# Values of two token blocks by seven quarter products, with running sums of queries, keys and values in PSUM

## What is computed

```python
qkv = x @ w_qkv.T                       # 512 -> 3 * 512
q, k = q*cos + rotate_half(q)*sin, k*cos + rotate_half(k)*sin
keep = (rel >= 0) & (rel < 64)          # window
out = softmax(where(keep, q @ k.T * scale, -inf)) @ v @ w_out.T
x = layernorm(x + out)
fuse = silu((x @ w_gate) * s_gate) * ((x @ w_up) * s_up)
x = layernorm(x + (fuse @ w_down) * s_down)
```

## Time and profile before

| | us |
|---|---|
| median of 3 runs | 1167.48 |
| the three runs | 1166.87, 1167.51, 1167.48 |
| span of the profiled execution, from its first to its last instruction | 1164.2 |

### The profile page before, as it was taken

How to read it: one execution, slowest core, us unless ns; L and a number is a source line. 1 busy time by engine, 2 the same in 40 slices (tenths; PEclk the granted TensorE clock), 3 DMA queues, 4 the chain that set the end, 5 groups by cost and what they waited for, 6 DMA issues and landing times.

```text
span 1164.2 us, 25539 instructions
## 1 busy us (share of the span) xinstructions
PE 1154.0 (99%) x8433; PEld 567.9 (49%) x8433; DVE 984.6 (85%) x2821; ACT 584.4 (50%) x1640; POOL 587.3 (50%) x563
## 2 busy tenths in 40 slices
PE   9999999999999999999999999999999999999998
PEld 4344446444464444644455444554445444464444
DVE  7899998898987899879998899897898988986434
ACT  3953883048820588105880169701686027950330
POOL 0775684156731667326771367613676236752330
PEclk9999999999999999999999999999999999999999
DMA  9999786366562765617656096561964537734000
GB/s 295 173 175 252 137 166 160 66 88 137 111 149 55 110 131 107 145 41 128 132 97 141 37 146 119 101 132 46 155 123 88 131 63 137 120 73 109 19 2 36
DMA packets 352077, 134.80 MB, mean 116 GB/s; under 512 B 309840, under 2 KB 332496, under 8 KB 351952
## 3 DMA queue, kind: packets, MB, share of 16 engines
q1 hardware_dynamic: 334976, 106.86, 49.6%
q0 software_dynamic: 10560, 17.30, 5.1%
q10 hardware_dynamic: 6416, 9.00, 2.1%
HBM read 32.19 MB, written 8.39 MB: 35 GB/s over the span
## 4 chain that ended last, share of the span: by engine, by line
PE 97%; DVE 1%; ACT 1%; issue 1%; POOL 0%; POOLq 0%; DVEq 0%
PE bank L842 61%; PE bank L1058 18%; PE bank L848 10%; PE bank L984 3%; PE bank L964 2%; PE bank L864 1%; PE bank L1080 1%; ACT bank L1243 1%; PE bank L873 0%; PE bank L1069 0%; PE bank L948 0%; DVE wd L1373 0%; ACT wu L1186 0%; DVE ffn_tmp L1530 0%; ACT fuse L1186 0%
## 5 line engine op out<-in xcount | busy, mean ns | idle before, releaser
L842 PE MATMUL bank<-x1T,wg 128*128 128x512 f16 (+1 forms) x1032 | 242.5, 378 | 0.0
L842 PE MATMUL bank<-x1T,wu 128*128 128x512 f16 x1024 | 241.9, 379 | 0.0
L1243 ACT ACTIVATE bank<-bank,neg_max,qk_scale 128x128 f32<-128x128 f32 x512 | 220.5, 435 | 7.8 <-DVE neg_max L1558 6.1
L1058 PE MATMUL bank<-wd,fuse 128*128 128x512 f16 (+2 forms) x1056 | 222.7, 373 | 0.0
L660 POOL TENSOR_TENSOR fuse<-ffn_tmp,fuse 128x512 f16<-128x512 f32 x128 | 149.7, 1170 | 117.5 <-ACT fuse L1186 116.8
L742 POOL TENSOR_TENSOR fuse<-fuse 128x512 f16<-128x512 f32 x116 | 137.7, 1218 | 74.9 <-ACT fuse L1186 72.8
L1058 PEld LDWEIGHTS bank<-wd,fuse 128*128 128x128 f16 x1056 | 101.9, 98 | 118.0
L842 PEld LDWEIGHTS bank<-x1T,wu 128*128 128x128 f16 x1024 | 100.1, 98 | 120.7
L655 POOL TENSOR_TENSOR xT_sb<-probs,xT_sb 128x512 f16<-128x512 f32 x112 | 129.6, 1158 | 44.5 <-ACT xT_sb L1186 44.4
L842 PEld LDWEIGHTS bank<-x1T,wg 128*128 128x128 f16 x1032 | 96.3, 98 | 113.9 <-issue 4.0
L1196 ACT ACTIVATE ffn_tmp<-bank,tanh_scale 128x512 f32<-128x512 f32 x128 | 88.2, 689 | 100.0 <-PE bank L842 76.8
(11 more groups left out here) (235 smaller groups left out, 1621.5 us busy)
## 6 DMA issues: line engine op xcount, KB each, us to landing
v_cross<-v_own SPq DMA_DIRECT2D x64, 128.0 KB, 2.4
out<-x ACTq DMA_DIRECT2D x31, 256.0 KB, 2.0
xT_sb<-xT SPq DMA_DIRECT2D x30, 256.0 KB, 4.1
qkT<-x SPq DMA_DIRECT2D x28, 256.0 KB, 3.8
wg<-w_gate POOLq DMA_DIRECT2D x7, 1024.0 KB, 5.2
wu<-w_up POOLq DMA_DIRECT2D x7, 512.0 KB, 6.0
wqkv<-w_qkvT SPq DMA_DIRECT2D x8, 256.0 KB, 6.3
wg<-w_gate POOLq DMA_DIRECT2D x1, 2048.0 KB, 8.4
```

The lines of the kernel that those rows point to most:

```text
L842: last = pe.matmul(dst, lhsT, rhs, start=(i == 0), stop=(i == len(pairs) - 1))
L1058: last = pe.matmul(dst[:, cols], fuse[:, s, z, rows], wd[:, s, cols], start=(s == 0 and z == 0), stop=(s == STEPS - 1 and z == 1))
L1243: last = act.activation(unit, unit, ACT.Exp, bias=neg_max[:, s % 2, h // 3, h % 3:h % 3 + 1], scale=qk_scale[:, 2:3], accum_out=row_sum[:, ...
```

## The change

Values are now also done by pairs of blocks, seven quarter products of 256 columns for each pair (`values_first` to `values_fourth`), 14 for a tile in place of four plain products. The scheme needs the sums of x that queries and keys already have, and four sums of the value weights. One of them replaces a part of `wqkv` in place; the other three are made once by POOL, stored in a DRAM tensor, `kept_v_weights`, and loaded back by ACT in each tile into the part of `v_cross` that is free between two tiles (`load_v_weights`).

In both schemes some of the seven products now add onto what stands in the bank: PE makes a product, ACT copies it (`keep_first`, `keep_fifth`, `keep_sixth`, `keep_seventh`, and `keep_values_...` with the scale of the values), and the next product is added to it in PSUM. So for queries and keys ACT makes four copies for a pair instead of one, and DVE three sums instead of seven. For values ACT makes four half-width copies for a pair, DVE adds kept part and bank into float32 rows (`add_v`, rows in `y`, `ffn_tmp` and `v_cross`), ACT makes their high half from those rows (`keep_v`), and DVE the low half from rows and high half (`split_v`, both in SBUF). The gate product of step 0 waits for `add_v` 0 and 1, that of step 1 for all four. The first three value products are issued at the end of the body before (`begin_values`), in place of the first block's product. In `first` POOL makes the sums of x for both pairs and those of the weights. Names of sums in `x_sums` and `w_sums` only change places.

```diff
+
         def kept_products(i):
 
-            if i == 0:
-                return rope_other[0], rope_other[1], rope_other[3]
-            return y[:, 0, :], ffn_tmp[:, 0, :], ffn_tmp[:, 1, :]
+            return rope_other if i == 0 else [o_rows[:, n, :] for n in range(NB)]
...
+        def v_places(i):
+
+            front, back = bank32[2 * i], bank32[2 * i + 1]
+            return front[:, 0:HALF_EMB], front[:, HALF_EMB:], back[:, 0:HALF_EMB], back[:, HALF_EMB:]
...
             def cross_v(a, j):
+                if j == 0 and not (isinstance(a, int) and a == 0):
+                    wait(v_product[1], sp, a - 1, V_FOURTH)
+                    sp.sem_inc(passed, 1)
+                    sp.wait_ge(v_weights_kept, 3 * 16)
+                    sp.sem_inc(passed, 1)
                 wait(v_low, sp, a, j)
...
+            def lessen_v_weights():
+                low_left, low_right, high_left, high_right = v_quarters()
+                wait(v_done, pool, 0, NB - 1)
+                pool.tensor_tensor(low_right, low_right, low_left, ALU.subtract).then_inc(v_weights_lessened, 1)
+
+            def add_v_weights():
+                low_left, right_less_left, high_left, high_right = v_quarters()
+                second, third, fourth = (added_v_weights(n) for n in range(3))
+                wait(pv_done, pool, 0, STEPS - 1)
+                pool.wait_ge(v_weights_lessened, 1)
+                pool.tensor_tensor(second, high_right, right_less_left, ALU.subtract).then_inc(v_weights_added, 1)
+                pool.wait_ge(v_weights_added, 1)
+                pool.tensor_tensor(fourth, high_left, second, ALU.subtract).then_inc(v_weights_added, 1)
+                pool.tensor_tensor(third, second, low_left, ALU.subtract).then_inc(v_weights_in[0], 16)
...
-            def project_pair(a, i, first=False):
...
+            def pair_first(a, i):
                 front_low, front_high, back_low, back_high = x_quarters(i)
...
+                done(first_product, quarter(pair_banks(i)[2], front_low, low_even))
...
+            def pair_fifth(a, i):
+                low_even, odd_less_even, high_even, high_odd = w_quarters()
+                pe.wait_ge(w_summed, 4)
+                done(fifth_product, quarter(pair_banks(i)[1], x_sums(i)[:, 1, :, :], odd_less_even))
+
+            def pair_sixth(a, i):
+                wait(products_kept, pe, a - 1, 4 * turn_of(i))
+                done(sixth_product, quarter(pair_banks(i)[2], x_sums(i)[:, 2, :, :], w_sums[:, 1, :, :], True))
+
+            def pair_seventh(a, i):
+                wait(products_kept, pe, a - 1, 4 * turn_of(i) + 2)
+                done(seventh_product, quarter(pair_banks(i)[2], x_sums(i)[:, 0, :, :], w_sums[:, 2, :, :], True))
+
+            def pair_third(a, i):
+                low_even, odd_less_even, high_even, high_odd = w_quarters()
+                wait(products_kept, pe, a - 1, 4 * turn_of(i) + 1)
+                done(qk_done, quarter(pair_banks(i)[1], x_sums(i)[:, 3, :, :], high_odd, True))
+
+            def pair_fourth(a, i):
+                front_low, front_high, back_low, back_high = x_quarters(i)
+                wait(products_kept, pe, a - 1, 4 * turn_of(i) + 3)
+                done(qk_done, quarter(pair_banks(i)[2], back_high, w_sums[:, 0, :, :], True))
+
+            def project_pair(a, i):
                 for j in (2 * i, 2 * i + 1):
                     wait_xT(pe, a, j)
-                if i == 0:
-                    wait(proj_read, pe, a - 1, NB - 1)
-                elif first:
-                    wait(proj_read, pe, a - 1, 1)
-                else:
-                    wait(down_read, pe, a - 2, NB - 1)
-                done(first_product, quarter(front_even, front_low, low_even))
-                if first:
-                    project_o(a - 1, NB - 1, False)
-                    wait(proj_read, pe, a - 1, 2)
-                wait(x_summed, pe, a - 1, 3)
-                pe.wait_ge(w_summed, 3)
-                done(sixth_product, quarter(back_even, sums[:, 1, :, :], w_sums[:, 0, :, :]))
-                pe.wait_ge(w_summed, 4)
...
-            def project_v(a, j, ffn, parts=range(KC)):
...
+            def values_first(a, i):
+                front_low, front_high, back_low, back_high = x_quarters(i)
+                low_left, right_less_left, high_left, high_right = v_quarters()
+                wait(rope_read, pe, a, i)
...
+            def values_fifth(a, i):
+                low_left, right_less_left, high_left, high_right = v_quarters()
...
+                done(v_product[i], quarter(v_places(i)[1], x_sums(i)[:, 1, :, :], right_less_left))
+
+            def values_sixth(a, i):
+                wait(v_products_kept[i], pe, a - 1, 0)
+                wait(v_weights_in, pe, a - 1, 15)
+                done(v_product[i], quarter(v_places(i)[3], x_sums(i)[:, 2, :, :], added_v_weights(0), True))
...
+            def values_second(a, i):
+                front_low, front_high, back_low, back_high = x_quarters(i)
+                low_left, right_less_left, high_left, high_right = v_quarters()
+                done(v_product[i], quarter(v_places(i)[0], front_high, high_left))
...
+            def begin_values(a):
+                values_first(a, 0)
+                values_fifth(a, 0)
+                values_first(a, 1)
+
+            def project_values(a):
+                values_sixth(a, 0)
+                values_third(a, 0)
+                values_fifth(a, 1)
+                values_seventh(a, 0)
+                values_sixth(a, 1)
+                values_second(a, 0)
+                values_fourth(a, 0)
+                values_third(a, 1)
+                values_seventh(a, 1)
+                scores(a, 0, True)
+                scores(a, 1, True)
+                values_second(a, 1)
+                values_fourth(a, 1)
...
@@ -1114,18 +1243,27 @@
                     if s == 13:
                         project_o(a, 2, ffn)
                     if s == 14:
-                        project_v(a + 1, 0, True)
-                project_pair(a + 1, 1, True)
+                        for j in range(2, NB):
+                            wait_xT(pe, a + 1, j)
+                        wait(proj_read, pe, a, 1)
+                        pair_second(a + 1, 1)
+                wait(proj_read, pe, a, 2)
+                pair_first(a + 1, 1)
+                project_o(a, NB - 1, ffn)
+                wait(x_summed, pe, a, 3)
+                pe.wait_ge(w_summed, 3)
+                pair_fifth(a + 1, 1)
+                pair_sixth(a + 1, 1)
+                pair_third(a + 1, 1)
+                pair_seventh(a + 1, 1)
+                pair_fourth(a + 1, 1)
+                begin_values(a + 1)
...
@@ -1145,7 +1283,7 @@
                     if s >= 2:
                         wait(gated, pe, f, s - 2)
                     elif attn:
-                        wait(v_low, pe, a, 2 * s + 1)
+                        wait(v_added, pe, a - 1, 2 * s + 1)
...
             def keep_v(a, j, ffn):
                 if ffn:
                     wait(proj_done, act, a - 1, j)
-                if j == 0 and not ffn:
+                    wait(v_added, act, a - 1, j)
+                    done(v_high, copy(v_own[:, j, :, 0, :], v_rows(j).rearrange("p (h d) -> p h d", h=HEADS)))
+                    return
...
+            def keep_value_product(a, i, dst, src, n):
+                wait(v_product[i], act, a - 1, n)
+                done(v_products_kept[i], copy(dst, src, v_scale[:, 1:2]))
...
+            def load_v_weights(a):
+                wait(pv_done, act, a, STEPS - 1)
+                act.sem_inc(passed, 1)
+                act.wait_ge(v_weights_kept, 3 * 16)
+                done(v_weights_in, act.dma_start(v_cross[:, 1:NB, :, :, :].rearrange("p b h z d -> p b (h z d)").bitcast(F32),
+                                                 kept_v_weights), 16)
...
@@ -1281,10 +1457,13 @@
                         split_high(a, 3, ffn, range(2 * (s - 5), 2 * (s - 4)))
                 keep_probs_high(a, STEPS - 1, ffn)
                 split_high(a + 1, 0, True)
+                keep_first(a + 1, 1)
                 for j in range(2):
                     split_x1_high(a, j, ffn)
                 split_high(a + 1, 1, True)
-                keep_first(a + 1, 1)
+                keep_fifth(a + 1, 1)
+                keep_sixth(a + 1, 1)
+                keep_seventh(a + 1, 1)
...
                 if attn:
+                    keep_values_first(a, 0)
+                    keep_values_fifth(a, 0)
+                    keep_values_first(a, 1)
+                    keep_values_sixth(a, 0)
+                    keep_values_fifth(a, 1)
+                    keep_values_seventh(a, 0)
+                    keep_values_sixth(a, 1)
+                    split_high(a, 2, ffn)
+                    keep_values_seventh(a, 1)
+                    split_high(a, 3, ffn)
                     keep_v(a, 0, ffn)
-                    split_high(a, 2, ffn)
                     keep_v(a, 1, ffn)
```

(60 more changed lines are left out.)

215 lines of the change are left out of this document (126 added, 89 removed).

## The result

The changed kernel takes 1206.88 us, the median of four runs (1206.46 to 1211.86), against 1167.17 us for the kernel before beside it: a ratio of 1.0351 with an interval of 1.0334 to 1.0367. The profiled execution has a span of 1204.9 us against 1164.2, so the span is 40.7 us longer, where 18.5 were predicted.

What follows compares the result with a forecast made beforehand. PE, busy for 1154.0 of 1164.2 us, was taken as the bound. A tile: -1.64 + 3.7 + 0.3 = +2.36, seven +16.5, passage +2.0; with 3.3 us around the span, 1186.0 us, range 1166 to 1195.

Steps and rivals of the forecast that it cites:

- What PE saves: Value stage: 14 quarter products bring the first gate product 1.64 us earlier in a tile, 11.5 us in seven.
- Queries and keys: Products added onto ACT's copies in the same bank: wait of PE put at nothing, range 0 to 0.8 us.
- The value products themselves: Value stage: half-width copies of 0.38 us fit under products of 0.86, so no wait among the 14.
- The hand-over to the gates: Gate of step 1 waits for the last `add_v` behind ACT's and DVE's queues: 2.2 us of wait a tile.
- And POOL in the way: Both `split_v` on DVE run beside POOL's block splits: 1.5 us more, making the gate's wait 3.7 us.
- Later in the loop: Behind the gate's wait, DVE's lateness mostly fits the room left: 0.3 us a tile, range 0 to 1.5.
- The room in the loop: First gating had 3.3 us of room, just used up; scores had 1.6 us, all but some tenths used.
- Passage to tile 1: Shorter value product, wait for a bank and ACT's lateness in the last pair products: 2.0 us once, bounds 0 and 4.
- The gates don't wait: Rival, 15%: ACT splits block 3 earlier or DVE does its sums ahead, so no gate wait: 1158 us.
- The lag stays in the loop: Rival, 12%: DVE isn't back before the output projection, 1.5 us more in a tile: 1196 us.
- The two sides cancel: Rival, 8%: the gate's wait is only 1.5 to 2 us: 1166 to 1170 us.

Runs made afterwards that it cites:

- g3: Changed kernel with the values made again by four full products as before; only queries and keys keep the new running sums: 1174.5 us.
- g2: Changed kernel with ACT's `keep_v` 0 and 1 before the split of block 3, and POOL's low halves of blocks 2 and 3 held until both `split_v`: 1211.4 us.
- e4: Changed kernel with 15 matmuls into an unread bank on PE ahead of the wait at the gate of step 1: 1202.8 us.
- e1: Changed kernel with all four `add_v` on DVE ahead of the splits of values 0 and 1 and the score maxima: 1208.1 us.
- h1: Changed kernel reordered on DVE and ACT: score maxima before the value splits, later copies and splits of values 2 and 3 moved back: 1177.3 us.
- g1: Changed kernel with a fourth value product issued before the loop's turn, and ACT's first kept value product waiting for an earlier DVE sum: 1206.3 us.
- k3: Only queries and keys changed, first full value product early in the passage, ACT's x1 copies put between kept pair products, kept fifth before block 1's split: 1168.9 us.
- e2_halves_first: Changed kernel with ACT's `keep_v` 0 and 1 ahead of the split of block 3: 1195.8 us.
- h2_scores_first_edges: The reordered kernel h1 with the two edits of g1 at the loop's turn and the passage into tile 1 added: 1171.3 us.
- j2: Kernel with only queries and keys changed (g3), with the first full value product ahead of tile 0's last two weighings: 1174.5 us.

## Why the prediction was right or wrong

The direction was right, the size was not: the span grew by 40.7 us and not by 18.5, and the time, 1206.9, lies above the range. By the steps of the prediction:

- *What PE saves.* Right: 12.74 us from the first value product to the first gate of tile 7, as forecast, 1.64 less than before; quarters 0.86 us apart.
- *Queries and keys.* Right for the tiles: g3 has no wait between the pair products in any of the six.
- *The value products themselves.* "No wait among the 14" holds for the kept copies. The step overlooked the place of the loop's turn, between the third and the fourth, 3.8 us of idle time in five tiles; their value stages are 5.1 us longer than that of tile 7. ACT's copy at half width with a scale took 0.47, not 0.38, without harm.
- *The hand-over to the gates.* Right, link by link: block 0's copy was forecast to end 13.6 us after the first value product and ended at 13.64 (1007.03 + 0.62 - 994.01).
- *And POOL in the way.* The mechanism was right and g2 shows it alone; the term was 1.5 us and measured 0.96 (0.70 and 1.64), so the wait was 3.21 to 3.25 and not 3.7. The Trainium skill (SBUF — State Buffer, Who interferes with whom) says that a DVE instruction with two SBUF inputs contends with a GpSimd one that reads SBUF, that the port pair they share is an exclusive lock, and that the order of issue decides who is blocked; 0.70 for the one and 1.64 for the next, beside POOL operations of 1.2 us, agree with that.
- *Later in the loop.* This is the step that failed in the tiles: 0.3 us a tile was its term. It priced the wait as idle time alone, and put 0.3 us on what follows. In tile 7 PE came out of the wait at a granted clock of 0.58, which is largely the lower of its two levels, 1.2 GHz, after having been idle for 3.2 us; that cost 1.3 to 2.8 us in six of seven tiles. No row of before could show it, as PE never was idle in a tile there. The rest is the loop's turn. As means of the six tiles, -1.64 for the saving, 3.25 for the wait, 1.8 for the clock and 0.85 for the longer value stage make 4.26 of the 4.49 measured; 0.2 stay unassigned.
- *The room in the loop.* "3.3 us of room, just used up" held for the first gating even at the full clock: in e4 the gate product of step 2 doesn't wait (4.01 us from gate 1 to gate 2). What the slow clock hid in the changed kernel is the weighing. e1 and g2 show what the step missed: it followed the chain to the gate, and not the one through maxima and probabilities, which was 5 us late and, by h1's order, is what limits once the gate is free.
- *Passage to tile 1.* The other step that failed: forecast 2.0 with a bound of 4, measured 9.3. The wait for the bank was put at 0.7 us and took 2.2; PE's 4.0 us for ACT's first kept value product, which waits for DVE's last sum of the pair, were not in the sum (2.5 us of first gate in g1). It held the transposes of x1 to have 10 us to spare and POOL's weight sums to cost nothing, and asked neither what stands on ACT behind the kept seventh product (6 us in k3) nor what DVE does beside those sums (3.1 us more in three instructions). How the 9.3 divide among these in the changed kernel stays open.

Of the rivals, "The gates don't wait" names two remedies (ACT's split of block 3 earlier, or DVE's sums ahead) and promised 1158. e1 is the second of them; it did take the gate's wait away and gave 1208.1, since it left the maxima late. The first was not run. "The lag stays in the loop" came out nearest, with 1196, but that is luck: its waits at the output projection show in no run, and the lag in e1, g2 and e4 stands at scores and weighing. "The two sides cancel" leaves the passage's 2.0 us out of its sum.

## What to carry to other kernels

When products move to running sums, the work goes to the queues of the other engines; walk each queue past the new instruction to whatever else stands behind it, and ask which chain started there before, here the score maxima. Try an order of the old chain first and the new sums behind it before judging such a change: 30 of its 40 us went by order alone. Look, too, for every instruction of another engine that new work on POOL will run beside. And a wait of PE that is new should be priced with what its clock does afterwards, as well as with its own length.

## What the runs showed of the hardware

- TensorE's clock fell after an idle stretch of 3.2 us in six of seven tiles of the changed kernel and in four of six of g1_edges, and after 2.1 us in three of seven of e2_halves_first; the two products behind it took up to 3.59 and 3.02 us instead of 1.9. Matmuls into an unread place over the same time kept it at 1.00 (e4_filled).
- At a hardware loop's turn PE was idle for 0.6 to 1.1 us behind three quarter products issued ahead of it (2.6 us of work), for at most 0.2 us behind four (3.5 us) in g1_edges but once 0.7 in h2_scores_first_edges, and not at all behind the full product before.
- DVE instructions took longer beside POOL's: a `tensor_tensor` from SBUF 1.65 us where it took 0.69 once POOL was held back (e2_halves_first, g2_apart), and two copies and a scaling of x1 4.93 us where j2 had 1.82.
- A wait removed ahead of a later one gave nothing back in the whole: 7 us of idle time in g1 were worth 0.6 us, and the same edits 6 us once the chain was on time.
